# Four neighbouring chunks per load: a re-ordered set of row offsets in a DLRM interaction kernel

## What is computed

```python
x0 = embeddings                       # (batch, 32 fields, 16)
xk = x0
for W in (W0, W1, W2):                # (32, h, 64)
    xk = relu(einsum('bmd,bhd,mhk->bkd', x0, xk, W))
    outs.append(sum(xk, axis=2))
z = concatenate(outs, axis=1)         # (batch, 192)
h = concatenate([z, dense_ctx], axis=1)
h = maximum(h @ W_top1 + b_top1, 0)
h = maximum(h @ W_top2 + b_top2, 0)
y = h @ W_top3
```

## Time and profile before

| | us |
|---|---|
| median of 3 runs (697.3, 699.67, 700.25) | 699.67 |
| the profiled execution | 699.1 |
| its span, first to last instruction | 697.3 |
| PE busy (matmuls) | 581.6 (83%) |
| DVE busy | 569.7 (82%) |
| POOL busy | 453.7 (65%) |
| ACT busy | 231.7 (33%) |
| share of time of the 16 DMA engines on SP's queue | 57.1% |

### The profile page before, as it was taken

One profiled execution on the slowest core, in us unless ns is written; L12 is line 12 of the kernel. 1 busy time (PEld: TensorE's weight loads), 2 busy tenths in 40 slices (PEclk: granted clock), 3 DMA queues, 4 the chain that ended last, 5 costly groups with the idle time before them and its releaser, 6 DMA issues.

```text
span 697.3 us, 7219 instructions
## 1 busy us (share of the span) xinstructions
PE 581.6 (83%) x2752; PEld 199.7 (29%) x2752; DVE 569.7 (82%) x295; ACT 231.7 (33%) x425; POOL 453.7 (65%) x348
## 2 busy tenths in 40 slices
PE   0040788999899989999899979998999989999978
PEld 0010222223332323323332324232332333233424
DVE  0020899998899998898889898898889889999963
ACT  0100361433325162615224242616243331616031
POOL 6776016188966978487948888487948896636120
PEclk9995799999999999999999999999999999999989
DMA  5498639059591949368672949195855949193000
GB/s 152 153 392 313 259 136 351 1 174 363 174 360 36 379 151 378 127 213 324 249 285 90 398 129 394 63 329 206 310 224 158 377 148 386 24 384 124 1 0 0
DMA packets 54244, 151.95 MB, mean 218 GB/s; under 512 B 9697, under 2 KB 18913, under 8 KB 54210
## 3 DMA queue, kind: packets, MB, share of 16 engines
q1 hardware_dynamic: 46018, 149.39, 57.1%
q0 software_dynamic: 8192, 2.11, 2.4%
HBM read 147.26 MB, written 4.20 MB: 217 GB/s over the span
## 4 chain that ended last, share of the span: by engine, by line
POOL 43%; issue 29%; PE 17%; DVE 3%; ACT 3%; POOLq 2%; SPq 1%; DMA 1%; DVEq 0%
POOL emb L281 25%; POOL zg L293 18%; PE acc L474 15%; DVE zd L360 3%; POOLq L292 2%; ACT xk_sb L389 1%; ACT xk_ps L389 1%; DMA z2d_y<-dense_t_in 1%; PE mlp L515 1%; ACT relu_ab L396 0%; PE mlp L506 0%; PE mlp L507 0%; PE acc L482 0%; DVE zpart L340 0%; PE mlp L562 0%
## 5 line engine op out<-in xcount | busy, mean ns | idle before, releaser
L360 DVE TENSOR_TENSOR zd<-rolled,xk_ps 128x2048 f32<-128x2048 f32 x244 | 543.9, 2282 | 112.5 <-issue 41.8
L474 PE MATMUL acc<-zd,w_sb 128*64 128x512 f32 x1696 | 401.0, 605 | 60.1 <-issue 33.5
L293 POOL TENSOR_TENSOR zg<-rolled,xk_sb 128x1024 f32<-128x1024 f32 x88 | 208.9, 2379 | 152.9 <-ACT xk_sb L389 151.8
L281 POOL DMA_INDIRECT emb<-tables_in,index x256 | 244.5, 955 | 69.2 <-issue 64.6
L474 PEld LDWEIGHTS acc<-zd,w_sb 128*64 128x64 f32 x1696 | 116.3, 138 | 317.7 <-issue 218.9
L389 ACT ACTIVATE xk_ps<-acc 64x512 f32<-64x512 f32 x128 | 73.0, 570 | 104.9 <-issue 52.9
L474 PE MATMUL acc<-zg,w_sb 128*64 128x512 f32 x352 | 91.4, 597 | 14.9 <-POOL zg L293 14.4
L474 PE MATMUL acc<-zd,w 128*64 128x512 f32 x256 | 63.0, 612 | 37.4 <-issue 36.7
L389 ACT ACTIVATE xk_sb<-acc 64x512 f32<-64x512 f32 x128 | 75.7, 591 | 3.1
L396 ACT ACTIVATE relu_ab<-acc 128x512 f32<-128x512 f32 x48 | 28.7, 597 | 122.7 <-issue 72.1
L474 PEld LDWEIGHTS acc<-zg,w_sb 128*64 128x64 f32 x352 | 23.8, 136 | 70.7 <-POOL zg L293 35.6
(11 more groups left out here) (46 smaller groups left out, 69.9 us busy)
## 6 DMA issues: line engine op xcount, KB each, us to landing
rolled<-x_scratch SPq DMA_DIRECT2D x256, 512.0 KB
base<-x_scratch SPq DMA_DIRECT2D x16, 512.0 KB
emb<-tables_in,index POOLq DMA_INDIRECT x256
x_scratch<-emb SPq DMA_DIRECT2D x32, 128.0 KB
w_sb<-w_in SPq DMA_DIRECT2D x2, 512.0 KB
wt<-wtop_in SPq DMA_DIRECT2D x1, 512.0 KB
wt1a<-wtop_in SPq DMA_DIRECT2D x1, 256.0 KB
w<-w0a_in SPq DMA_DIRECT2D x1, 160.0 KB
```

What stands on the lines that cost most here:

```text
L281: pool.indirect_dma_start(emb[:, i % 2, c * DIM:(c + 1) * DIM], None, tables, bass.IndirectOffsetOnAxis(index[:, g:g + 1].bitcast(U32), 0) ...
L293: nc.gpsimd.tensor_tensor(zg[:, n % ZG_BUFS, :], rolled[:, s, j, :], xk_sb[:, s, :], ALU.mult).then_inc(zg_ready, 1)
L360: nc.vector.tensor_tensor(zd[:, n % ZD_BUFS, 0:w, :], rolled[:, s, j:j + w, :], repeated(xk_ps[:, s, :], w), ALU.mult).then_inc(zd_ready, 1)
L474: end = nc.tensor.matmul(acc[h * MAPS:(h + 1) * MAPS, s, :], weights, z[:, h * HALF:(h + 1) * HALF], start=(i == 0 and c == 0), stop=(i == ...
```

## The change

The scratch and its rows stay as they are; what changes is which fields stand in a chunk, and how many chunks one DMA brings.

- A partition's field becomes (1 + j + 4 (p%4) + p//4) mod 32: the four residues of p are now 4 rows apart instead of 1, and chunk j starts at row 1 + j. For a partition, chunk j+1 is then the row behind chunk j. The chunks 0 to 3 still hold the offsets 1 to 16 that layer 0 needs. `layout` orders the weights in the same way.
- One DMA loads `LOAD` = 4 chunks: each partition reads 16 KB in one piece. A slot has 4 semaphores instead of 16.
- SP waits before each such DMA for every product of (i-2, 2) that reads one of its four chunks, and takes the groups in the order in which they come free.
- DVE and POOL wait for the group in which their chunk lies.

```diff
-BASES = [1, 5, 9, 13, 0, 2, 3, 4, 6, 7, 8, 10, 11, 12, 14, 15]
+FIRST_BASE = 1
+STEP = 4
 L0CH = 4
+LOAD = 4
+def load_order(users):
+    def freed(j):
+        return max([k for k, (_, _, first, w) in enumerate(users) if first < j + LOAD and j < first + w], default=j)
+    return sorted(range(0, NCH, LOAD), key=freed)
-        rolled_in = [[sem(f"rolled_{'ab'[s]}{j}_in") for j in range(NCH)] for s in range(2)]
+        rolled_in = [[sem(f"rolled_{'ab'[s]}{j}_in") for j in range(NCH // LOAD)] for s in range(2)]
-            def rows_from(first, i, step):
+            def rows_from(first, i, step, w):
                 return bass.AP(scratch.tensor, scratch.offset + (i * ROWS + first) * COLS,
-                               [[COLS, FIELDS], [step * COLS, GROUPS], [1, COLS]])
+                               [[COLS, FIELDS], [step * COLS, GROUPS], [1, w * COLS]])
-                order = PLAN.merged[phase_of(i - 2, 2) if i > 1 else phase_of(i, 1)]
-                for who, n, first, w in order:
-                    if i > 1:
-                        sp.wait_ge(zd_ready if who == "dve" else zg_ready, n + 1)
-                    for j in range(first, first + w):
-                        sp.dma_start(rolled[:, s, j, :], rows_from(BASES[j], i, 1)).then_inc(rolled_in[s][j], 16)
+                users = PLAN.merged[phase_of(i - 2, 2)] if i > 1 else []
+                for j in load_order(users):
+                    for who, n, first, w in users:
+                        if first < j + LOAD and j < first + w:
+                            sp.wait_ge(zd_ready if who == "dve" else zg_ready, n + 1)
+                    sp.dma_start(rolled[:, s, j:j + LOAD, :], rows_from(FIRST_BASE + j, i, STEP, LOAD)
+                                 ).then_inc(rolled_in[s][j // LOAD], 16)
-                    pool.wait_ge(rolled_in[s][j], 16 * (stream // 2 + 1))
+                    pool.wait_ge(rolled_in[s][j // LOAD], 16 * (stream // 2 + 1))
-                    for c in range(j, j + w):
-                        if layer == 0 or (layer == 1 and c >= L0CH):
+                    if layer == 0 or (layer == 1 and j >= L0CH):
+                        for c in range(j // LOAD, (j + w - 1) // LOAD + 1):
                             dve.wait_ge(rolled_in[s][c], 16 * (stream // 2 + 1))
-    base = np.array(BASES)
-    m = (base[:, None] + p[None, :] % 4 + p[None, :] // 4) % FIELDS
+    base = FIRST_BASE + np.arange(NCH)
+    m = (base[:, None] + STEP * (p[None, :] % 4) + p[None, :] // 4) % FIELDS
```

More of the change, by code:

```diff
@@ L237, in load_stream @@
                     sp.wait_ge(squares_ready, i)
-                sp.dma_start(base[:, :], rows_from(0, i, 0)).then_inc(base_in, 16)
-                order = PLAN.merged[phase_of(i - 2, 2) if i > 1 else phase_of(i, 1)]
-                for who, n, first, w in order:
-                    if i > 1:
-                        sp.wait_ge(zd_ready if who == "dve" else zg_ready, n + 1)
-                    for j in range(first, first + w):
-                        sp.dma_start(rolled[:, s, j, :], rows_from(BASES[j], i, 1)).then_inc(rolled_in[s][j], 16)
+                sp.dma_start(base[:, :], rows_from(0, i, 0, 1)).then_inc(base_in, 16)
+                users = PLAN.merged[phase_of(i - 2, 2)] if i > 1 else []
[5 more added lines that the diff above has]
+                                 ).then_inc(rolled_in[s][j // LOAD], 16)
             sp.dma_start(ids_sb[:, 0:1 + GATHERS], ids[:, 0:1 + GATHERS]).then_inc(first_ids_in, 16)
```

## The result

| us | before | changed |
|---|---|---|
| median of 20 runs each | 698.57 | 701.49 |
| lowest, highest | 697.3, 700.69 | 698.36, 703.32 |
| ratio, 95% interval | | 1.0037, 1.0026 to 1.0048 |
| the profiled execution (span) | 699.1 (697.3) | 703.11 (701.3) |

The changed kernel is 0.37% slower, 2.6 us by the ratio and 2.9 us by the medians. The kernel before has a median of 698.57 over 20 runs, where the forecast started from the 699.67 of three.

A forecast was written before the change was run, and what follows sets the result against it. PE and DVE in lock step were taken to bound the kernel. First load +2.3 us, hidden; other loads, issues and rate 0 each: 699.7 us, the median before being 699.67; range 696 to 706.

The forecast's parts named there:

- The bound and the steady state: Middle of the kernel: PE and DVE in lock step set the 76.85 us period; later loads arrive in time, cost 0.
- SP's 192 saved issues: SP's queue: sixteen issues become four per stream, worth 0 because SP waits for gathers afterwards in any case.
- The room of 5.8 us for an odd stream: Steady loads: an odd stream's first group lands at 312.1, DVE wants it at 317.9, so 5.8 us are left.
- The rate: Loads of `rolled` with 16 KB rows: taken near 375 GB/s, possibly as low as 247; cost 0.
- the fourth rival: All loads: 16 KB rows are slow, below 239 GB/s loads set the period; at 200 GB/s +104, about 804; 4%.
- the fifth: Loads: 16 KB rows are cut into 4 KB packets again, rate unchanged; 699.7, chance included in the forecast's 67%.
- The first load: Program's start: both first products wait for the whole group, so (0,0) is made 2.3 us later, hidden in ACT's gap.
- They cost nothing as long as the end of the gap does not depend on them.: Head: the 2.3 us delay lies inside ACT's idle gap, 24.5 us of it behind PE's work, and costs 0.
- an end fixed by something else: Head: the forecast's case, ACT starts again at 68.5 despite the 2.3 us delay; 699.7 us, 67%.
- the first rival: Head: ACT's gap has a fixed length behind PE's last matmul, so the +2.3 us get through; 702.0, 9%.
- The rival on the loads of stream 1 (711.3): Head: ACT's gap ends with stream 1's load, moving from 68.50 to 80.1; +11.6 us, or +6 if third group; 11%.
- the one in which the gap goes away (678.0): Head: many short queued loads make the gap; without them ACT starts at 46.8, everything behind 21.7 us sooner; 9%.

The follow-up runs named there:

- the run that only waits: The kernel before with its 16 loads unchanged, but DVE's first product also waits for chunk 3: 702.14 against 698.81 us, ratio 1.0055.

## Why the prediction was right in its number and wrong in its likeliest case

**The bound and the steady state: right.** The forecast said that no phase after the head waits for a load, that the period stays at 76.85 us and that SP's 192 saved issues are worth nothing. The period is 76.94 (the next one of the same trace 76.87), and DVE's only wait for `rolled` is the first. The room of 5.8 us for an odd stream was tested from the outside: with groups of eight it is used up and one wait of 1.06 us appears, with sixteen the period grows by 11.5 us.

**The rate: right in sign, and the doubt was not needed.** 403 GB/s, where 375 was taken and down to 247 allowed. The Trainium skill's rule ("DMA: Bandwidth & Descriptors", "Rules for kernel authors", at least 1 MiB in one DMA) agrees with this row. The change made the DMAs and their rows longer together, and no run tells which of the two does it; the new addresses alone, at 373 GB/s, don't. As foreseen, the faster loads reach the end nowhere. With 403 GB/s the fourth rival falls, and with 18370 packets instead of 46018 the fifth.

**The first load: the mechanism right, the term too small.** The prediction put (0,0) 2.3 us later; PE's last matmuls of it end 3.3 us later, 47.30 against 44.04. Two things were mis-sized. First, it counted the delay of the second product. But PE's first matmul starts 2.43 us behind the first product in both traces, and the last ends 7.3 and 7.4 us behind that, so what counts is the first product, and that was to be 36.97 - 34.31 = 2.7 us late by the prediction's own rows. Second, the group landed later than the fourth single chunk: 11.1 us after the issue of `base` instead of 10.5, so the first product was 3.2 us later (2.7 for the second). How much of the second part is the group's own is not shown. The three traces of the changed kernel have it 11.1, 11.4 and 11.9 us behind `base`, the traces with single chunks have the fourth of them 10.0 to 11.3 us behind it.

**The step that failed: "They cost nothing as long as the end of the gap does not depend on them."** It does depend on them: ACT starts 3.3 us later, 71.82 against 68.50, which is over the 3 us by which the prediction itself wanted to be called wrong. The forecast gave 67% to an end fixed by something else and 9% to a gap of fixed length behind PE. The argument against the latter, that no other hand-over from PE to ACT takes 24 us, was no argument: a gap without a named cause is as odd with one anchor as with another. With the first rival's own sum, 699.7 + 2.3 = 702.0, the number would have been 0.5 us off. Part of that, and of the 1.8 us by which the forecast itself missed, is luck: the median of the kernel before came out 1.1 us under the 699.67 that the sums start from. As a difference, the forecast had 0 and its first rival 2.3 us, and 2.9 were measured. Nor does the first rival hold to the letter: over all runs the gap behind PE's last matmul is 23.3 to 26.1 us, and its length is steadier from PE's first. The cost is under 3.5 us either way, which is why the chance of 76% for no difference of over 0.5% was fair and the range held.

**The rival on the loads of stream 1 (711.3) and the one in which the gap goes away (678.0)** both fall: the run that only waits moves ACT by some 2 to 2.6 us with no load changed, with eight chunks in a load ACT starts earlier and not later (66.22), and in the changed kernel the gap is as long as before. The second has a strange echo: the gap does go away, with 25 us, but with the chip and not with the kernel.

## What to carry to other kernels

A merged load costs nothing where nobody waits for a load, and here it gained nothing there either; it costs where somebody waits: at the first use. Merge the steady loads and keep the first one cut at what the first instruction reads; here two DMAs instead of one for one stream of 16 took back the whole loss. And an idle stretch without a cause on the path between a delay and the end is not cover: until a run has moved its start and left its end where it was, count the delay in full.

## What was not expected of the hardware

- Whole chips differ by 25 us of about 700 on this program, by one gap: on one, ACT takes `acc` 0.04 us after PE's last matmul of (0,0), and the kernel before takes 673.5 us; on the others 23 to 26 us pass, and it takes 698.3 to 698.8. PE's mean granted clock goes with it (0.990 to 0.995 in the traces without the gap, 0.973 to 0.978 in those with it, leaving out the run with sixteen chunks per load). But in the kernel before, PE's clock is still granted at 1.00 (2.4 GHz) from 44 to 48 us, when PE is already idle, at 0.80 from 48 to 50 and at 0.50 (1.2 GHz) from 50 us on. The low clock comes behind the beginning of the gap, so it is a result of it as far as the rows show.
- Loads of 2.1 MB with rows of 16 KB instead of 0.5 MB with rows of 4 KB raise the rate of the same queue from 375 to 403 GB/s. SP issues the four loads of a stream in some 3 us at the start, where the 16 took 19 and 22 us. The 16 are issued that slowly only in the head, and only in the traces with the gap: on the chip without it SP needs 11.2 to 11.6 us for the first stream's 16, and in the middle of the kernel before 11.1 us. What makes SP slower there, no run tells.
